# DLRM tower with a CIN recommender: 26 of 47 product tiles split, 14 of their low parts made on GpSimd, five transposes per group

## What is computed

```python
e = jnp.stack([tbl_0[ids[:, 0]], ..., tbl_38[ids[:, 38]]], axis=1)   # (2048, 39, 16)
for idx, (W, b) in enumerate(((w0, b0), (w1, b1), (w2, b2))):       # 128 maps each
    z = jnp.einsum('bhd,bkd,hks->bsd', x0, xk, W) + b[None, :, None]
    z = jax.nn.relu(z)
    if idx != n_layers - 1:
        xk = z[:, :64, :]
        direct.append(z[:, 64:, :])
    else:
        direct.append(z)
logit = jnp.sum(jnp.concatenate(direct, axis=1), axis=-1)            # (2048, 256)
h = jnp.maximum(jnp.concatenate([logit, dense_ctx], axis=1) @ W_top1 + b_top1, 0.0)
h = jnp.maximum(h @ W_top2 + b_top2, 0.0)
y = h @ W_top3
```

## Time and profile before

| | us |
|---|---|
| median of 3 runs | 2676.76 |
| lowest and highest | 2674.07, 2679.92 |
| the profiled execution | 2672.68 |
| its span in the trace | 2670.9 |
| DVE busy | 2491.4 (93%) |
| PE busy | 2504.7 (94%) |
| POOL busy | 958.3 (36%) |
| ACT busy | 917.8 (34%) |

### The profile page before, as it was taken

How to read it: one execution, slowest core, us unless ns; L and a number is a source line. 1 busy time by engine, 2 the same in 40 slices (tenths; PEclk the granted TensorE clock), 3 DMA queues, 4 the chain that set the end, 5 groups by cost and what they waited for, 6 DMA issues and landing times.

```text
span 2670.9 us, 28197 instructions
## 1 busy us (share of the span) xinstructions
PE 2504.7 (94%) x7622; PEld 1401.1 (52%) x7622; DVE 2491.4 (93%) x2409; ACT 917.8 (34%) x885; POOL 958.3 (36%) x674
## 2 busy tenths in 40 slices
PE   0489999999999999999999999999999999999988
PEld 0245555555555555555555555555555555555546
DVE  2389999999999999999999999999999999999982
ACT  0133333333333333333333333333333333333325
POOL 6671451807244270715426072532607163000000
PEclk9899999999999999999999999999999999999999
DMA  3887889978787998878789887878988787888710
GB/s 72 202 197 182 202 187 215 207 183 203 179 202 179 216 198 195 196 179 199 178 206 197 199 200 179 197 176 203 196 205 201 180 199 180 202 195 198 175 47 9
DMA packets 165360, 488.34 MB, mean 183 GB/s; under 512 B 31730, under 2 KB 48227, under 8 KB 165331
## 3 DMA queue, kind: packets, MB, share of 16 engines
q1 hardware_dynamic: 141997, 480.37, 77.1%
q0 software_dynamic: 19968, 5.15, 1.7%
q10 hardware_dynamic: 3367, 2.48, 0.3%
HBM read 465.35 MB, written 22.55 MB: 183 GB/s over the span
## 4 chain that ended last, share of the span: by engine, by line
DVE 36%; PE 26%; DMA 16%; issue 15%; SPq 3%; ACT 2%; POOL 1%; DVEq 1%; ACTq 0%; POOLq 0%
DVE prod L696 18%; DMA spread<-x_periods 14%; PE zacc_a L802 10%; PE zacc_b L802 10%; DVE low L668 9%; DVE prod L684 6%; SPq L417 2%; POOL landed L476 1%; PE zacc_a L837 1%; PE zacc_b L837 1%; DMA shifted<-x_periods 1%; DVE half L703 1%; ACT high L569 1%; ACT maps L541 1%; ACT maps L540 1%
## 5 line engine op out<-in xcount | busy, mean ns | idle before, releaser
L696 DVE TENSOR_TENSOR prod<-spread,maps 128x1024 f32<-128x1024 f32 (+1 forms) x1280 | 1502.5, 1218 | 50.4 <-DMA spread<-x_periods 47.7
L569 ACT ACTIVATE high<-prod 128x1024 fp32r<-128x1024 f32 (+2 forms) x576 | 608.6, 1057 | 1400.8 <-DVE prod L696 1168.7
L476 POOL DMA_INDIRECT landed<-in_tbl,rows_id x624 | 938.7, 1504 | 239.2 <-issue 234.2
L802 PE MATMUL zacc_a<-prod,w_plain 128*128 128x512 f32 (+2 forms) x1856 | 852.7, 594 | 33.6 <-DVE prod L696 17.6
L802 PE MATMUL zacc_b<-prod,w_plain 128*128 128x512 f32 (+2 forms) x1856 | 850.4, 593 | 5.3 <-DVE prod L696 5.3
L668 DVE TENSOR_TENSOR low<-prod,high 128x1024 fp32r<-128x1024 f32 (+1 forms) x512 | 624.9, 1221 | 0.0
L802 PEld LDWEIGHTS zacc_a<-prod,w_plain 128*128 128x128 f32 (+2 forms) x1856 | 351.1, 190 | 360.7 <-issue 329.1
L802 PEld LDWEIGHTS zacc_b<-prod,w_plain 128*128 128x128 f32 (+2 forms) x1856 | 351.7, 190 | 331.8 <-issue 293.3
L482 POOL TENSOR_TENSOR mark<-mark 128x1 f32<-128x1 f32 x30 | 15.9, 530 | 1033.8 <-PE maps L850 1032.6
L684 DVE TENSOR_TENSOR prod<-shifted,x_thrice 117x1024 f32<-117x1024 f32 (+1 forms) x224 | 265.1, 1218 | 43.9 <-DMA shifted<-x_periods 42.9
L837 PE MATMUL zacc_b<-low,w_high 128*128 128x512 f32 (+1 forms) x512 | 235.1, 540 | 19.9 <-DVE low L668 19.8
(11 more groups left out here) (101 smaller groups left out, 895.7 us busy)
## 6 DMA issues: line engine op xcount, KB each, us to landing
spread<-x_periods SPq DMA_DIRECT2D x640, 512.0 KB, 20.8
shifted<-x_periods SPq DMA_DIRECT2D x192, 468.0 KB
x_periods<-x SPq DMA_DIRECT2D x32, 624.0 KB
x_thrice<-x_periods SPq DMA_DIRECT2D x96, 156.0 KB
landed<-in_tbl,rows_id POOLq DMA_INDIRECT x624
shifted<-x_periods SPq DMA_DIRECT2D x32, 312.0 KB
features<-feat ACTq DMA_DIRECT2D x16, 128.0 KB, 7.4
spread<-features SPq DMA_DIRECT2D x4, 512.0 KB, 5.4
```

The source lines that it names most:

```text
L476: nc.gpsimd.indirect_dma_start(out=landed[:, f, :], out_offset=None, in_=tables[f], in_offset=bass.IndirectOffsetOnAxis(ap=rows_id[:, f:f ...
L569: nc.scalar.activation(high[0:rows, h, :], prod[0:rows, p, :], ACT.Copy).then_inc(s_round, 1)
L696: nc.vector.tensor_tensor(to, spread[0:rows, t, :], maps[0:rows, :], ALU.mult).then_inc(s_prod, 1)
L802: return nc.tensor.matmul(z[:, hf * BANK:(hf + 1) * BANK], w, x[:, hf * BANK:(hf + 1) * BANK], start=start, stop=stop)
```

## The change

PLAN gets a third letter: in a tile P the low part is made by POOL instead of DVE, otherwise it is as V. There are now 21 F, 12 V and 14 P; `high` has 4 buffers. POOL does the P tiles in the order of the tiles, and the gathers are put between them, one behind every second tile from tile 21 of the even turn on, the last three behind tile 46 of the odd one. `turn_x` takes a whole group at once: five transposes of 128 columns of `landed`, at tile 13 of the even turn; ACT copies at 15, SP writes at 16, and POOL renews `rows_id` at 20. `x_periods` has rows of 128 numbers and only two periods in place of four, and a `shifted` tile is loaded by three DMAs of 39 rows. At the start POOL waits only for the first ids, the first two pieces of `spread` are loaded before the start-up SQUARED, and the others right behind it rather than behind the loads for the turn after.

```diff
-PERIODS = 4
+PERIODS = 2
-PLAN = "FVFFVFFVFFVFFVFVFVFV" "FVFVFVF" "FVFFVFFVFFVFFVFFFVFV"
-NP, NH = 8, 3
+PLAN = "FPVFPFVPFFPVFPVFPVFV" "FPFVPFF" "FPVFPFVPFVPFFPFFPVFV"
+SPLIT = "VP"
+NP, NH = 8, 4
-TURN_AT = (4, 9)
-COPY_AT = (6, 11)
-WRITE_AT = (7, 12)
-GATHER_AT = 12
+TURN_AT, COPY_AT, WRITE_AT, GATHER_AT = 13, 15, 16, 20
+FIRST_PIECES = 2
...
             def load_shifted(n, u):
-                rows = rows_of(N1 + u)
-                sp.dma_start(shifted[0:rows, u % RING0, :], period(n, PER0 * u, rows)).then_inc(s_shifted[u], 16)
+                for s in range(rows_of(N1 + u) // FIELDS):
+                    sp.dma_start(shifted[s * FIELDS:(s + 1) * FIELDS, u % RING0, :], period(n, PER0 * u, FIELDS)
+                                 ).then_inc(s_shifted[u], 16)
...
                 if turn.fixed and turn.number() == -1 and j == 0:
                     write_x(nxt)
+                    load_first(nxt)
+                    sp.wait_ge(s_prep, 1)
+                    for q in range(FIRST_PIECES):
+                        load_spread(nxt, q)
...
+            def low_part(turn, j):
+                rows, at_ = rows_of(j), slot(j, ALL, NP)
+                pool.wait_ge(s_round, n_kind(turn, j, SPLIT) + 1)
+                nc.gpsimd.tensor_tensor(low[0:rows, at_, :], prod[0:rows, at_, :], high[0:rows, slot(j, SPLIT, NH), :],
+                                        ALU.subtract).then_inc(s_lowp, 1)
...
-                    pool.wait_ge(s_first, 32)
-                    gather()
-                    later(turn.shift(3), 1)
-                fetched = turn.shift(4)
-                if j == GATHER_AT and not turn.odd and fetched.real():
-                    later(fetched, fetched.group(1, 0))
+                    pool.wait_ge(s_first, 16)
+                    gather(0, FIELDS)
+                    pool.wait_ge(s_all, 16)
+                    numbers(turn.shift(3), 1)
+                    gather(0, 12)
+                if PLAN[j] == "P" and has(turn, j):
+                    low_part(turn, j)
...
+                    for f in range(FIELDS):
+                        if min(GATHER_AT + 1 + 2 * f, 2 * TILES - 1) == turn.odd * TILES + j:
+                            gather(f, f + 1)
...
-                pe.wait_ge(s_lowv, n_kind(turn, j, "V") + 1)
+                pe.wait_ge(*low_done(turn, j))
...
-                for d in range(CHAN):
-                    done = nc.tensor.transpose(maps2[0:FIELDS, d * ROWS:(d + 1) * ROWS],
-                                               landed[:, :, n.odd * CHAN + d], ident[:, :])
+                flat = landed[:, :, :].rearrange("p f d -> p (f d)")
+                for q in range(TURNED):
+                    n_ = min(128, FLAT - q * 128)
+                    done = nc.tensor.transpose(maps2[0:n_, q * ROWS:(q + 1) * ROWS], flat[:, q * 128:q * 128 + n_],
+                                               ident[:, :])
```

More of the change, by code:

```diff
@@ L220, in build @@
         s_turned = sem("s_turned")
-        s_pad = sem("s_pad")
         s_x = sem("s_x")
-        s_written = [sem(f"s_written{n}") for n in range(2)]
+        s_written = sem("s_written")
         s_thrice = sem("s_thrice")
@@ L263, in n_kind, with low_done @@
             return turn.count(rank(TILES, kinds), at_start + rank(j, kinds))
+        def low_done(turn, j):
+            return (s_lowv if PLAN[j] == "V" else s_lowp), n_kind(turn, j, PLAN[j]) + 1
         def n_tile(turn, j, plus=0):
@@ L274, in tail @@
         def tail(of):
-            split = [j for j in of if PLAN[j] == "V"]
+            split = [j for j in of if PLAN[j] in SPLIT]
             return split[-1] if split and split[-1] + LATE >= of[-1] else None
@@ L382, in _ @@
                              ).then_inc(s_wload, 16)
+            whole = (TURNED - 1) * 128
             def group_of(n):
@@ L431, in emit @@
                     load_shifted(nxt, u)
+                if turn.fixed and turn.number() == -1 and j == SQUARED[-1]:
+                    for q in range(FIRST_PIECES, PIECES):
+                        load_spread(nxt, q)
                 if j == SQUARED[-1] and after.real():
@@ L472, in _, with gather @@
             nc.gpsimd.memset(mark[:, :], 0.0).then_inc(s_mark, 1)
-            def gather():
-                for f in range(FIELDS):
+            def gather(first, last):
+                for f in range(first, last):
                     nc.gpsimd.indirect_dma_start(
@@ L482, in touch, with numbers @@
                 nc.gpsimd.tensor_tensor(mark[:, 0:1], mark[:, 0:1], mark[:, 1:2], ALU.add).then_inc(s_mark, 1)
-            def later(n, group):
-                pool.wait_ge(s_turned, n.count(1, 0))
+            def numbers(n, group):
+                pool.wait_ge(s_turned, n.group(1, 0))
                 pool.wait_ge(s_mark, n.group(2, -1))
@@ L554, in emit @@
                 if turn.fixed and turn.number() == -1 and j == 0:
[L555 removed]
                     copy_x(nxt)
[L557 removed]
                     act.wait_ge(s_const, 16 * 4)
[L559 to L560 removed]
+                if PLAN[j] in SPLIT and has(turn, j):
+                    h, p, rows = slot(j, SPLIT, NH), slot(j, ALL, NP), rows_of(j)
                     if j in SQUARED:
@@ L570, in emit @@
                                          ).then_inc(s_round, 1)
-                if j in COPY_AT and not turn.odd and turn.shift(2).real():
-                    copy_x(turn.shift(2 + COPY_AT.index(j)))
+                if j == COPY_AT and not turn.odd and turn.shift(2).real():
+                    copy_x(turn.shift(2))
                 if nxt.real() and j == N1 + N0 - 1 + LZ:
@@ L664, in low_part @@
                 rows = rows_of(j)
-                whole, top = prod[0:rows, slot(j, ALL, NP), :], high[0:rows, slot(j, "V", NH), :]
-                dve.wait_ge(s_round, n_kind(turn, j, "V") + 1)
-                to = high[HALF:128, slot(j, "V", NH), :] if stacked(j) else low[0:rows, slot(j, ALL, NP), :]
+                whole, top = prod[0:rows, slot(j, ALL, NP), :], high[0:rows, slot(j, SPLIT, NH), :]
+                dve.wait_ge(s_round, n_kind(turn, j, SPLIT) + 1)
+                to = high[HALF:128, slot(j, SPLIT, NH), :] if stacked(j) else low[0:rows, slot(j, ALL, NP), :]
                 nc.vector.tensor_tensor(to, whole, top, ALU.subtract).then_inc(s_lowv, 1)
@@ L863, in emit @@
                     then = step_back(turn, j, LATE)
-                    if then and PLAN[then[1]] == "V":
+                    if then and PLAN[then[1]] in SPLIT:
                         done = contract_low(*then)
@@ L878, in emit @@
                         done.then_inc(s_mm, 1)
-                if j in TURN_AT and not turn.odd and turn.shift(2).real():
-                    turn_x(turn.shift(2 + TURN_AT.index(j)))
+                if j == TURN_AT and not turn.odd and turn.shift(2).real():
+                    turn_x(turn.shift(2))
             turns(pe, emit)
```

112 lines of the change are left out of this document (58 added, 54 removed).

## The result

The changed kernel takes 2837.45 us (median of 4 runs, 2835.56 to 2839.76) against 2678.34 for the kernel before (median of 4, 2674.07 to 2682.41): a ratio of 1.0595, 95% interval 1.0574 to 1.0615. It is slower by 6%, where the forecast was 2612.

The account below looks back on a forecast made before the run. DVE was taken as the bound by 1 to 2 us, PE right behind. From 2672.7 us, 50 for the turns and 15 for the start came off: 2608, plus 4 for the median, 2612; range 2520 to 2740.

Parts of the forecast that it names:

- DVE's own work: DVE per turn: six subtractions fewer take 6.8 us off 76.3, leaving 69.5 us.
- POOL's subtraction: One P tile's low part on POOL: 2.4 us taken, between a low end of 1.22 and a high end of 3.7.
- Exclusive turns both ways: POOL and DVE exclude each other by whole instructions wherever DVE reads both operands from SBUF.
- Five meetings of 1.2 us, 6.1 per turn: DVE held by POOL's subtractions five times per turn, 1.2 us each on average, 2.35 for tile 21; 6.1 us.
- my walk: Tile-by-tile pass through one turn at 1.13 us per DVE instruction, placing POOL's subtractions; it found five meetings, 6.1 us.
- The turn is the larger of DVE's 75.6 and PE's 72.0: Whole turn: DVE's 69.5 plus 6.1 exceeds PE's 72.0, so the turn is 75.6 us, 1.6 less than before.
- ACT makes 8 more high parts, this costs nothing: ACT's added `high` parts leave it under 72 us per group, free while DVE and PE need over 140.
- The start: Before the steady turns: earlier gathers and early `spread` pieces save 15 us, between 0 and 25.
- The marks I set: Signs in the start: first PAIRED product before 100 us and turn 1's SQUARED before 145.
- C: Rival: POOL becomes the bound; 2767 us at 80.6 per turn, 2680 at 77.8, over 3000 with 3.7 us subtractions; chance 0.32.
- My list of signs: Trace signs for forecast and rivals, among them DVE gaps of about 1 us or DVE instructions longer than 1.22.
- B: Rival: DVE goes first or meetings are rare, so PE is the bound at 73 us per turn; 2532 us; chance 0.20.

Follow-up runs that it names:

- e2: Changed kernel with POOL's subtractions kept, but PE reads `high` in place of their low parts and only buffers wait for POOL; 2893.17 us.
- e1: Changed kernel with POOL's 14 subtractions per turn left out; PE reads `high` once more in place of those low parts; 2621.96 us.
- e12: Changed kernel with POOL's subtractions left out; PE reads constant weights in place of those low parts; 2624.64 us.
- e13: e12 with the second P of SQUARED at tile 25 instead of 24; 2592.75 us.
- e14: Changed kernel with the second P of SQUARED at tile 25 instead of 24; 2833.39 us.
- e3: Changed kernel with the old PLAN (18 V, no P) and three `high` buffers, keeping all other edits; 2662.81 us.
- e8: Changed kernel with POOL's subtractions made but unread; PE reads constant weights instead and only buffers wait for POOL; 2898.25 us.

## Why the prediction was wrong, point by point

**DVE's own work: right.** 69.5 was summed and 69.7 measured; over all kernels the sums 76.3, 69.5, 74.0, 71.8, 72.9 and 85.3 meet 76.3, 69.7, 74.0, 71.7, 72.7 and 85.0.

**POOL's subtraction: right.** 2.4 was taken, 2404 ns is the median. (By the Trainium skill, "GPSIMD Engine Reference", section "Performance versus the Vector engine", the estimate was 2.25, half of its 4497 ns for twice the columns; the trace is 7% above it.)

**Exclusive turns both ways: right in kind.** e2 against e1 shows that POOL's instructions hold DVE, the row at 1377.54 that they do so until their end. (The Trainium skill, "Trainium Architecture — The Big Picture", section "What this means for kernel authors", calls the port pair that DVE and GpSimd share an exclusive lock and no split of bandwidth; the trace agrees: 2.44 us for a step of 0.29.)

**Five meetings of 1.2 us, 6.1 per turn: too small.** Measured 8.4. I had walked through the turn with POOL's subtractions in time and booked about two meetings at summing steps; the six steps alone cost 5.0 us (2.17 + 1.80 + 1.07), since a step of 0.3 us is held as long as one of 1.2 (by 2.15 at 1377.54, the subtraction at 1317.90 by 2.0), and three steps one product apart can be met by two subtractions in a row (the first `half` at 1373.26 took 1.76 us for 0.68, `sums` at 1377.54 2.44). With this term right and the rest as predicted, the turn would have been 69.5 + 8.4 = 77.9 and the time 2672.7 + 31 x 0.7 - 15 + 4 = 2683, no gain but no loss of 6% either. SQUARED, which I booked at 2.35 for tile 21, costs 2.5 over seven products. `low`, two to three meetings in my walk, is only 0.9.

**"The turn is the larger of DVE's 75.6 and PE's 72.0": the step that failed.** With nothing held the turn is 75.8 (e12) and 75.2 (e13), not 72.0 or 73: PE is busy for 73 us and has gaps of 2.5, in which it waits for `high` and `low`, and DVE waits 5.3 to 5.9 us, most of it for PE's buffers. That alone is as long as my forecast with the meetings in. And the held time doesn't vanish in this slack. With 8.4 us held DVE needs 78.1 and PE 75.2, but the turn is 82.5: DVE's waits shrink only from 5.9 to 4.3, and PE's gaps grow from 2.6 to 7.2. PE's busy time grows too, from 73.2 to 75.2 with the same matmuls, at a granted clock of 0.96 instead of 0.99. My reading is that what holds DVE also makes `high` and `low` late for PE. How much of PE's gaps comes by that way and how much by buffers and low parts that wait for POOL itself isn't separated: of PE's waits 27 us are for POOL's low parts directly, and ACT waits 12.6 us for POOL to free `high`. In the sum of the turn, 69.7 + 8.4 + 4.3 = 82.5 against 69.5 + 6.1 = 75.6, 2.3 of the missing 6.9 us are held time, 4.3 are waits booked at nothing and 0.2 is DVE's own work. e14 shows that one can't take the two terms apart either: 2 us less of waiting was 2.5 us more of holding.

**"ACT makes 8 more high parts, this costs nothing": wrong in one place.** By load it is right (ACT 41% busy). By order it is not: `high` of tile 24 stands behind the three takes of layer 1 on ACT, where V's letters in the old SQUARED avoided it, and PE waits 2.5 to 2.7 us there. e13 removes that gap. Its price includes the clock, which falls behind such a gap; see the last section.

**The start: right for the edits, not for the kernel.** 15 was booked; e3 gains 17.8 at the first take and e12 17.3, the changed kernel 5.7. The other 12 us go to POOL's subtractions up to that take, since e12 differs only in these and in what PE reads in their place. The marks I set (first PAIRED product before 100, SQUARED of turn 1 before 145) came at 107.8 and 138.5, so one was missed and one met.

**The rivals.** C named POOL as the bottleneck with 2767 at most, or over 3000. It was right that the kernel gets slower, but not by its mechanism: POOL is busy for 61.6 us per turn of 82.5 (1679.85 of 2250 us) and for 81% of the stretch with gathers from 1321 to 1449, not over 90%; it waits 422 us for `high` itself; PE's waits for its low parts are 27 of some 204 us; and turns 29 and 30, where no gathers are left, are still 81.7 and 81.8. (The page's chain that ended last does lead through POOL for 25% of the span, where it had 1%; but e12 and e2 with e8 show that what costs is POOL's instructions beside DVE's and not their results.) Two sums in C were off: 155 per group is 77.6 per turn, not 77.8, and with a subtraction of 3.7 the group would ask for 125 + 28 x 1.3 + 30 = 191, not 180. B is what e12 shows, except that it ends at 75.8 and not at 73. My list of signs did name the true one, DVE instructions longer than 1.22.

**A pause of POOL that I had not booked.** Once in some 485 us (before: 460) POOL stands still ahead of a gather, for 9.1 us at the longest. Before, nobody waited for it; now PE and DVE do:

```profile
768.17 0.94 POOL L490 DMA_INDIRECT landed<-in_tbl,rows_id  x1 [9.12 <-issue]
...
771.53 1.22 PE L869 MATMUL zacc_b<-low,w_high 128*128 128x512 f32 x2 [4.64 <-POOL low L512]
...
772.79 2.34 DVE L728 TENSOR_TENSOR prod<-spread,maps 128x1024 f32<-128x1024 f32 x2 [6.35 <-PE zacc_b L869]
```

That turn has 90.0 us and the one with the pause at 1256.25 has 87.2, beside some 82.2 for most: 13 us in these two.

## What to carry to other kernels

In this kernel work given to GpSimd was paid for wherever VectorE read two operands from SBUF, by the whole GpSimd instruction, even if VectorE's own step was tiny (2.44 us for 0.29); count the places free of such instructions first, and give GpSimd only as much as fits there (with six to nine of 47 tiles the kernel was 0.9 to 1.8% faster than before, of which 0.6% came from the other edits, e3; with fourteen it lost 6%). Where two engines are within 5% of each other and feed each other through a few buffers, don't take the larger sum for the turn: find the pace of the pair with the disputed cost left out (e12), and add delays to that. When a step is added to an engine with much idle time, look at what stands directly ahead of it in that engine's order.
